# A four-layer network's attention keys: turned and split into three parts one stage earlier

## The chip, the cores and the metric

The kernel runs on 1 core of one Trainium2 chip. The metric is device time in microseconds (us), the median of several executions. Work goes to five engines: TensorE (PE, its weight loads apart as PEld), VectorE (DVE), ScalarE (ACT), GpSimd (POOL) and SyncE (SP), which here only issues transfers. Each engine runs its own instructions in the order in which they are written, and waits on semaphores for the others.

## The reference, cut to what matters

x is 4 batches of 512 rows of 256 numbers. Four layers follow one another, each an attention over a context of 1601 rows and a feed-forward part.

```python
x = x + tanh(g_xattn[0]) * L0_xattn(layernorm(x), ctx)
x = x + tanh(g_ffn[0]) * quantised_linear(layernorm(x))
x = x + tanh(g_xattn[1]) * L1_xattn(layernorm(x), ctx, mask)      # keys and queries turned (RoPE)
x = x + tanh(g_ffn[1]) * L1_experts(layernorm(x))                 # 8 experts, relu
x = x + tanh(g_xattn[2]) * L2_xattn(layernorm(x), ctx, mask)
x = x + tanh(g_ffn[2]) * L2_experts(layernorm(x))                 # gelu
x = x + tanh(g_xattn[3]) * L3_xattn(layernorm(x), ctx)            # one wide head
x = x + tanh(g_ffn[3]) * L3_experts(layernorm(x))                 # selu, two experts a row
# attention of layers 1 and 2: 16 heads of 16
q, k, v = x @ Wq + bq, ctx @ Wk + bk, ctx @ Wv + bv
k = k * cos + rotate_half(k) * sin                                # layer 1 alone; q alike
attn = softmax(where(mask == 0, -big, q @ k.T * scale))
out = (attn @ v) @ Wo + bo
```

Keys and values hang on the context and on weights alone, so they can be computed before the layer that uses them begins.

## The kernel before

**Stages.** Each stage ends in a fence and its buffers are given back. In the profiled execution layer 1's stages are: the quantised linear part of layer 0 (928 to 1087 us), layer 1's attention (1087 to 2112), its experts (2112 to 2421), and then layer 2's attention (2421 to 3302).

**Keys made ahead.** `Prepared` belongs to a feed-forward stage. It projects keys and values of the next layer in 16 chunks of the context (4 batches of 512, 512, 512 and 65 columns; a chunk gives two pieces of keys of 128 rows, so 32 pieces in all). SP loads the context (L201), PE projects (L218 keys, L226 values), ACT moves the keys from PSUM to a ring of three buffers `p_kf` (L243) and stores them as float32 in DRAM (`keys`, L246). The chunks are put in parts; each engine's code names the place at which a part comes. `quantised_linear` has ten parts of one to seven chunks, the experts have three.

**Attention of layers 1 and 2** (`ready`). Scores are made in PE from bf16 operands: a float32 number is written as the sum of three bf16 parts (`split3`, four operations: L835 to L838), and the parts of q and k stand under one another in the rows of `qaug` and `kaug` (six runs of 16 rows, then four rows of mask, maximum and ones). So each piece of keys is loaded from `keys` (L725), and in layer 1 once more from `turned`, a copy in DRAM with the halves of each head swapped (L750, L778); POOL or DVE turns it (three operations, L860 to L862, with the table `turn`) and splits it; SP stores the three parts in `kparts` (L794), and only then fetches a group's operands to `kaug` (L816, six transfers of 16 partitions) and `qaug`.

**Groups and batches.** The 16 heads form four groups (g = 0 to 3) for each of four batches (b). `Plan` lays the order of all engines out as a list. `attend(g, b)` makes the 52 jobs of one group (13 key tiles times 4 heads: L1051 scores, L1143 exponential on ACT, L1062 product with v) and mixes into them what comes next: `maxima`, the pass over the scores for the maximum of each row (L1032 on PE, L930 on DVE, 32 steps a group, two groups ahead), `project` (queries L1007 and, before the change, all keys of the next batch, in groups 1 and 2), `fetch`, `take`, `normalise` and `output`. The end of a group is the copy `z<-pv` on ACT (L1150).

Of the kernel before, what the change touches and what calls it, by code (L numbers as in the profile page):

```python
# [14 lines left out]
H, HD = 16, 16  # L15
# [136 lines left out]
class Prepared:  # L152
# [3 lines left out]
    def __init__(self, kn, sb, w, slots, *counts):  # L156
        self.w, self.slots = w, slots
        self.wk, self.wv, self.bk = sb("p_wk", [P, DC, D]), sb("p_wv", [P, DC, D]), sb("p_bk", [P, DC])
        self.at, self.kf = sb("p_ctx", [P, 4, DC, 512]), sb("p_kf", [P, 3, 512])
        self.vb = sb("p_vb", [P, 2, 4, D])  # L160
        self.chunks, s, k = [], 0, 0
        for b in range(B):
            for n_c, (c0, n) in enumerate(CHUNKS):
                c = dict(b=b, n_c=n_c, i=len(self.chunks), keys=[], values=[])
                for j in range(DC):
                    c["keys"].append((j, s, k))
# [5 lines left out]
                self.chunks.append(c)  # L172
        self.n, self.n_keys = s, k
        self.parts, first = [], 0
        for n in counts:
            self.parts.append(self.chunks[first:first + n])
            first += n
        self.parts.append(self.chunks[first:])
        self.loaded = 0

    def ended(self, part):

        return self.parts[part][-1]["end"]


def prepare_weights_sp(kn, p):
# [18 lines left out]

def prepare_pe(kn, p, part):
# [3 lines left out]
    for c in p.parts[part]:  # L210
# [3 lines left out]
        for j, s, _ in c["keys"]:  # L214
# [16 lines left out]
def prepare_act(kn, p, part):  # L231
    act, p_full, p_free, p_w = kn.nc.scalar, kn.sema("p_full"), kn.sema("p_free"), kn.sema("p_w", DMA)
    keys, values = kn.dram["keys"], kn.dram["values"]
    many = len(p.slots)
    act.wait_ge(p_w.sem, p_w.at(3))
    for c in p.parts[part]:
        c0, n = CHUNKS[c["n_c"]]
        for j, s, k in c["keys"]:
            kept = kn.sema(f"p_k{k % 3}", DMA)
# [3 lines left out]
            act.activation(p.kf[:, k % 3, 0:n], p.slots[s % many][:, 0:n], ACT.Identity,  # L243
                           bias=p.bk[:, j:j + 1]).then_inc(p_free.sem, 1)
            act.wait_ge(p_free.sem, p_free.at(s + 1))
            act.dma_start(keys[c["b"], P * j:P * j + P, c0:c0 + n], p.kf[:, k % 3, 0:n]).then_inc(kept.sem, DMA)  # L246
# [11 lines left out]

def prepare_close(kn, p):

    n = len(p.chunks)
    for name, k in (("p_full", p.n), ("p_free", p.n)):
        kn.sema(name).close(k)
    kn.sema("p_w", DMA).close(3)
    for f in range(4):
        kn.sema(f"p_ctx{f}", DMA).close(n // 4)
    names = []
    for k in range(3):
        kn.sema(f"p_k{k}", DMA).close(len(range(k, p.n_keys, 3)))
        names.append(f"p_k{k}")  # L270
    for k in range(2):
# [22 lines left out]
class Unit:  # L294
# [13 lines left out]
    at: int = 0  # L308


class Plan:
# [16 lines left out]
    def add(self, kind, **f):  # L328
# [3 lines left out]
        if kind in ("q", "k"):  # L332
            if kind == "q" or not self.ready:
                u.s = self.next("s", 2 if self.rope else 1)
# [3 lines left out]
            u.at = self.next(f"kl{u.f}") if kind == "k" and self.ready else -1  # L338
# [34 lines left out]
    def split(self, kind, b, c, n_c, engines):  # L373
        n = self.next("split")
        self.add(kind, b=b, j=c, k=n_c, by=engines[n % len(engines)], f=n % (3 if n < 10 else 2))
# [86 lines left out]
    def lay_out_ready(self):  # L462
        lead, n = self.lead, 0
        self.add("begin", b=0, what="kvq")
        for n_c in range(len(CHUNKS)):
            for c in range(DC):
                self.split("k", 0, c, n_c, ("pool",) if n < (4 if self.rope else 5) else ("dve",))
                n += 1
        self.add("ln")
        for c in range(DC):  # L470
            self.split("q", 0, c, 0, ("pool",) if self.rope else ("dve",))
        for g in range(NG):
            self.add("fetch", b=0, g=g, what="k", k=1, by=f"kd{g}")
            if g == 0:
                self.add("fetch", b=0, g=0, what="q", k=NG, by="qd")
# [7 lines left out]
        self.attend(0, 0, (self.chain(self.maxima(1, 0, lead), self.maxima(2, 0, 0, lead)), MAX_STEPS, 0, JOBS - 1))  # L483
        for b in range(B - 1):
            peaks = (self.chain(self.maxima(2, b, lead), self.maxima(3, b), self.maxima(0, b + 1), self.maxima(1, b + 1),
                                self.maxima(2, b + 1, 0, lead)), MAX_STEPS, 0, JOBS - 1)
            projected = self.chain(self.project(b + 1, ("pool", "pool", "dve") if self.rope else ("pool",), "kvq"),
                                   *(self.then("fetch", b=b + 1, g=g, what="kq", k=1, by=f"kd{g}") for g in (0, 1)))
            self.attend(1, b, peaks, (projected, 6, 0, JOBS - 1), (self.normalise(0, b), 2, 2 * HG, JOBS - 1))
            self.attend(2, b, peaks, (projected, 6, 0, 36), (self.normalise(1, b), 2, 2 * HG, JOBS - 1))  # L490
            self.attend(3, b, peaks, (self.chain(self.then("fetch", b=b + 1, g=2, what="kq", k=1, by="kd2"),
                                                 *(self.then("take", b=b + 1, g=g) for g in range(3))), 4, 8, 24),
                        (self.normalise(2, b), 2, 2 * HG, JOBS - 1))
            self.attend(0, b + 1, peaks, (self.chain(self.then("fetch", b=b + 1, g=3, what="kq", k=1, by="kd3"),
                                                     self.then("take", b=b + 1, g=3)), 2, 8, 24),
                        (self.chain(self.normalise(3, b), self.output(b)), 2 + TT + 1, 2 * HG, JOBS - 1))
        peaks = (self.chain(self.maxima(2, B - 1, lead), self.maxima(3, B - 1)), MAX_STEPS, 0, JOBS - 1)
        for g in range(1, NG):
            self.attend(g, B - 1, peaks, (self.normalise(g - 1, B - 1), 2, 2 * HG, JOBS - 1))
# [13 lines left out]
def head_attention(kn, w, gate, scale, rope, mask, ready):  # L513
# [3 lines left out]
    with ctx:  # L517
# [8 lines left out]
        if rope is not None:  # L526
            a.wqr, a.bqr = sb("wqr", [P, DC, D]), sb("bqr", [P, DC])
            a.turn = sb("turn", [P, 2, 2, 512])
# [23 lines left out]
        if ready:  # L552
            a.fill = sb("fill", [R_ALL - R_MASK, S2], BF16)
            third = sb("third", [P, 3, 512], BF16)
# [5 lines left out]
        a.split_at.append((a.e_t[:, 0, 0, :], a.e_t[:, 0, 1, :], third[:, :, :]))  # L560
# [33 lines left out]
def head_sp(kn, a):  # L594
# [7 lines left out]
    turned = [sig(f"turn{f}", DMA) for f in range(2)]  # L602
# [3 lines left out]
    a.ctx_of, a.turn_of, a.arrived, a.stored_of = {}, {}, {}, {}  # L606
    ctx_until, turn_until = [None] * 4, [None] * 2
# [96 lines left out]
def head_ready_sp(kn, a, n_of):  # L704
# [4 lines left out]
    stored = [sig(f"stored{f}", DMA) for f in range(3)]  # L709
    turned = [sig(f"turn{f}", DMA) for f in range(2)]  # L710
    split = {n: sig("split_" + n) for n in ("pool", "dve")}
    v_taken, vl, swapped = sig("v_taken"), sig("vl", DMA), sig("swapped", DMA)
    keys, turn_keys, values = kn.dram["keys"], kn.dram["turned"], kn.dram["values"]
# [1528 lines left out]
```

## Time and profile before

| | |
|---|---|
| median of 3 executions | 4383.25 us (4382.84 to 4405.29) |
| the profiled execution's own time | 4430.76 us |
| its span | 4429.5 us |
| mean granted clock of PE | 0.903 of full speed |
| PE busy | 3646.0 us (82%) |
| DVE busy | 2172.4 us (49%) |
| ACT busy | 2069.1 us (47%) |
| POOL busy | 722.6 us (16%) |

The span is the stretch that the trace covers; the time is the same execution's from outside. Busy time of an engine says how much it has to do, the waits say who sets the pace at a place.

### The profile page before, as it was taken

To read this page: it belongs to the slowest core of one execution; us is meant where nothing else is said; L and a number is where in the kernel's file an instruction comes from. 1 tells how busy PE (TensorE), PEld (TensorE's weight loads), DVE (VectorE), ACT (ScalarE), POOL (GpSimd) and SP (SyncE) were. 2 spreads that over 40 slices of the span, in tenths; PEclk is the share of its full clock that TensorE was granted. 3 is DMA by queue.
4 is the path that set the end of the run, shared out by engine and by line. 5 is a ranking of instruction groups with operands and counts; after the bars stand their busy time and mean duration, and the time that the engine had idled before them with its cause. 6 is when DMAs were issued, how large, how long until landed. Compare 5 with 4: busy or idle time off the path is not lost. (4 is left out here: it accounts for less than half of the span.)

```text
span 4429.5 us, 54375 instructions
## 1 busy us (share of the span) xinstructions
PE 3646.0 (82%) x19494; PEld 1930.1 (44%) x19494; DVE 2172.4 (49%) x3371; ACT 2069.1 (47%) x4542; POOL 722.6 (16%) x732
## 2 busy tenths in 40 slices
PE   3999999988187879799898498898988978893993
PEld 2334343345022323233696133332337855583993
DVE  4766666632285767674202676676731121252332
ACT  1566666643034546466232165565653322252662
POOL 1112120011423131200202130312001100003013
PEclk8999999999578989899898598998999999996997
DMA  6242415034644343420755624434117521022555
GB/s 129 42 61 48 69 41 67 1 131 152 154 90 73 73 74 69 81 29 1 259 184 160 108 66 54 90 67 67 16 60 246 167 97 55 17 90 94 180 181 105
DMA packets 255284, 415.17 MB, mean 94 GB/s; under 512 B 51578, under 2 KB 169043, under 8 KB 252971
## 3 DMA queue, kind: packets, MB, share of 16 engines
q1 hardware_dynamic: 207714, 273.76, 29.1%
q0 software_dynamic: 27360, 98.58, 7.2%
q10 hardware_dynamic: 19944, 39.36, 2.3%
q8 instruction: 159, 2.61, 0.3%
q14 instruction: 107, 0.87, 0.1%
HBM read 305.62 MB, written 111.08 MB: 94 GB/s over the span
## 5 line engine op out<-in xcount | busy, mean ns | idle before, releaser
L1143 ACT ACTIVATE e_t<-s 128x512 f32<-128x512 f32 (+1 forms) x2496 | 1355.0, 599 | 981.3 <-PE s L1051 980.3
L930 DVE TENSOR_REDUCE mxp<-m 128x1 f32<-128x802 f32 x1536 | 1451.8, 987 | 666.0 <-PE m L1032 661.0
L1032 PE MATMUL m<-kaug,qaug 97*128 97x401 bf16 x3072 | 839.5, 357 | 281.4 <-DMA qaug<-qparts 91.7
L1051 PE MATMUL s<-qaug,kaug 100*128 100x512 bf16 (+1 forms) x2496 | 881.3, 394 | 34.3 <-DMA qaug<-tm 19.5
L1062 PE MATMUL pv<-e_t,v 128*32 128x512 f32 (+1 forms) x4992 | 686.3, 623 | 0.2
L1032 PEld LDWEIGHTS m<-kaug,qaug 97*128 97x128 bf16 x3072 | 281.8, 101 | 699.4 <-DVE mxp L930 253.3
L1051 PEld LDWEIGHTS s<-qaug,kaug 100*128 100x128 bf16 (+1 forms) x2496 | 238.9, 102 | 730.0 <-ACT e_t L1143 474.5
L1952 PE MATMUL y<-w,hT 128*128 (+1 forms) x1504 | 346.6, 385 | 11.6 <-DVE hT L1807 11.6
L1952 PEld LDWEIGHTS y<-w,hT 128*128 128x128 f32 x1504 | 283.2, 193 | 48.7 <-issue 6.4
L1943 PE MATMUL h<-xtT,w 128*128 128x128 f32 x2496 | 293.4, 276 | 4.8 <-issue 3.5
L1943 PEld LDWEIGHTS h<-xtT,w 128*128 128x128 f32 x2496 | 286.6, 193 | 6.1 <-issue 3.9
L893 POOL TENSOR_TENSOR r<-ones,rc 128x512 f32<-128x512 f32 x48 | 50.3, 1048 | 1343.6 <-DVE rc L952 1343.6
L1812 DVE SCALAR_TENSOR_TENSOR y<-y,b 128x256 f32<-128x256 f32 x94 | 39.5, 420 | 358.1 <-PE y L1952 358.1
L1062 PEld LDWEIGHTS pv<-e_t,v 128*32 128x32 f32 (+1 forms) x4992 | 99.5, 109 | 225.1 <-ACT e_t L1143 146.1
L2020 ACT ACTIVATE ez<-h,b 128x128 f32<-128x128 f32 x440 | 119.8, 387 | 158.2 <-PE h L1943 158.2
L1806 DVE TENSOR_SCALAR ez<-ez 128x1024 f32<-128x1024 f32 x55 | 38.2, 694 | 299.4 <-ACT z L2020 299.4
L836 POOL TENSOR_TENSOR kr<-kf,ks 128x512 f32<-128x512 f32 (+1 forms) x91 | 92.5, 1016 | 366.4 <-ACT ks L1119 361.3
L2025 ACT ACTIVATE hT<-h,b 128x128 f32<-128x128 f32 x312 | 84.7, 382 | 125.2 <-PE h L1943 125.1
L1767 POOL DMA_DIRECT2D w<-in_L_w x78 | 55.3, 708 | 504.8 <-PE h L1943 479.2
L2020 ACT ACTIVATE z<-h,b 128x128 f32<-128x128 f32 x440 | 122.5, 453 | 0.0
L218 PE MATMUL h<-p_ctx,p_wk 128*128 128x512 f32 (+1 forms) x256 | 107.7, 569 | 15.7 <-DMA p_ctx<-in_ctxT 14.6
L226 PE MATMUL h<-p_wv,p_ctx 128*128 128x256 f32 (+1 forms) x416 | 102.7, 397 | 20.7 <-ACT p_kf L243 11.6
(288 smaller groups left out, 3405.0 us busy)
## 6 DMA issues: line engine op xcount, KB each, us to landing
w<-in_L_w POOLq DMA_DIRECT2D x78, 1024.0 KB, 5.4
kaug<-kparts SPq DMA_DIRECT2D x276, 200.1 KB
kparts<-ks SPq DMA_DIRECT2D x66, 384.0 KB, 3.5
w<-in_L_w SPq DMA_DIRECT2D x24, 1024.0 KB, 13.3
p_ctx<-in_ctxT SPq DMA_DIRECT2D x36, 512.0 KB
keys<-p_kf ACTq DMA_DIRECT2D x72, 256.0 KB
values<-p_vb ACTq DMA_DIRECT2D x36, 512.0 KB
qaug<-qparts SPq DMA_DIRECT2D x216, 64.0 KB
```

The lines of the kernel that those rows point to most:

```text
L218: m = pe.matmul(p.slots[s % many][:, 0:n], p.wk[:, kc, P * j:P * j + P], p.at[:, f, kc, 0:n], start=kc == 0, stop=kc == DC - 1)
L226: m = pe.matmul(p.slots[s % many][0:KW[t], 0:D], p.at[:, f, kc, k0:k0 + KW[t]], p.wv[:, kc, :], start=kc == 0, stop=kc == DC - 1)
L836: kn.settle(eng, own, eng.tensor_tensor(rest, src, parts[0], ALU.subtract))
L930: dve.tensor_reduce(a.mxp[:, u.g % 2, half, n:n + 1], a.m_slot[u.m % 2][:].rearrange("p (a n) -> p a n", a=2)[:, :, 0:PIECE + 1], AX.XY, A ...
L1032: m = pe.matmul(slot[:, 512 * k:512 * k + PIECE + 1], a.qaug[0:R_MAX, u.g, j, P * qc:P * qc + P], a.kaug[0:R_MAX, u.g, j, k0:k0 + PIECE + ...
L1051: pe.matmul(slot[0:KW[u.k], :], a.kaug[0:R_ALL, u.g, u.j, P * u.k:P * u.k + KW[u.k]], a.qaug[0:R_ALL, u.g, u.j, :], start=True, stop=True) ...
L1062: m = pe.matmul(a.pv[32 * j:32 * j + 32, :], a.v[0:KW[u.k], u.k, u.g, VW * j:VW * j + 32], a.e_t[0:KW[u.k], u.n % 2, j, :], start=u.k == 0 ...
L1143: act.activation(a.e_t[0:KW[u.k], e % 2, u.j, :], a.s_slot[u.s % 3][0:KW[u.k], :], ACT.Exp).then_inc(s_free.sem, 1)
L1943: m = pe.matmul(a.h_slot[i % 2][:, P * f:P * f + P], a.w1[:, w1_at, c, P * f:P * f + P], xT(c), start=c == 0, stop=c == DC - 1)
L1952: m = pe.matmul(a.y_slot[i % 2][:, 0:D], a.hT[:, i % 2, f, :], w2(f), start=f == 0, stop=f == FC - 1)
L2020: t = act.activation(to[:, p, P * f:P * f + P], slot[:, P * f:P * f + P], func, bias=bias(f))
L2025: t = act.activation(a.hT[:, p, f, :], slot[:, P * f:P * f + P], func, bias=bias(f))
```

## The change

The turn and the split move from the attention of layers 1 and 2 into the stage ahead of each. There ACT evicts keys to a ring of four and no longer stores them. For layer 1 SP swaps halves from `p_kf` to `p_kr` within SBUF (L236 of the changed kernel), POOL and DVE turn and split in `prepare_split` (L335 to L337 and L876 to L879, seven operations a piece), and SP stores the three parts to `kready` (L242). So that halves are 64 partitions each, the columns of Wk are permuted on the host; the fetch to `kaug` then takes pieces of 8 partitions in layer 1 (twelve transfers of a group) and stays at six of 16 in layer 2. For layer 2 there is no turn, and ACT writes the first part. The 42 transfers that clear `xs` come six after each part instead of all at once. In the attention the key loads, turns, splits, stores and the swapped copies in DRAM are gone; each group's operands of the next batch are fetched and taken within the next group (`renew`), and queries alone are projected, on POOL's split.

```diff
@@ Prepared, prepare_sp (new: a part at a time)
-def prepare_sp(kn, p, upto):
+def prepare_sp(kn, p, part):
...
+    def swap(x):
+        swapped = kn.sema(f"p_sw{x['k'] % p.RING}", DMA)
+        sp.wait_ge(p_free.sem, p_free.at(x["s"] + 1))
+        f, n = x["k"] % p.RING, x["cols"]
+        for r in (0, P // 2):
+            sp.dma_start(p.kr[r:r + P // 2, f, 0:n], p.kf[P // 2 - r:P - r, f, 0:n]).then_inc(swapped.sem, DMA)
+
+    def store(x):
+        split, kept = kn.sema("p_split_" + x["by"]), kn.sema(f"p_k{x['k'] % p.RING}", DMA)
+        sp.wait_ge(split.sem, split.at(x["n"] + 1))
...
+    for c in p.parts[part]:
+        prepare_load_sp(kn, p, min(c["i"] + 4, len(p.chunks)))
+        if p.in_parts:
+            for x in c["keys"]:
+                if p.rope is not None:
+                    swap(x)
+                held.append(x)
+                if len(held) > 2:
+                    store(held.pop(0))
+    for x in held:
+        store(x)
@@ prepare_act
-            if k >= 3:
-                act.wait_ge(kept.sem, kept.at(k // 3))
+            if k >= p.RING:
+                act.wait_ge(kept.sem, kept.at(k // p.RING))
@@ prepare_split (new, on POOL and DVE)
+        if p.rope is not None:
...
+            eng.tensor_tensor(src, src, p.turn[:, 0, c0:c0 + n], ALU.mult)
+            kn.settle(eng, own, eng.tensor_tensor(o, o, p.turn[:, 1, c0:c0 + n], ALU.mult))
+            kn.settle(eng, own, eng.tensor_tensor(src, src, o, ALU.add))
+        split3(kn, eng, own, kn.cst["ones"][:, 0:1].to_broadcast([P, n]), o, src, [p.ks[:, f, k, 0:n] for k in range(3)],
+               p.rope is None).then_inc(done.sem, 1)
@@ quantised_linear, quant_sp, quant_dve
+        both = ("pool", "dve")
+        a.p = Prepared(kn, sb, ahead, [s[:] for s in a.p_slot], True, rope,
+                       ((1, ("pool",)), (1, ("pool",)), *((1, both) for _ in range(7)), (7, both)))
-    for n in range(XTILES):
-        sp.dma_start(kn.dram["xs"][P * n:P * n + P, :], a.zero[:]).then_inc(zeroed.sem, DMA)
-    prepare_sp(kn, a.p, len(a.p.chunks))
+    for part in range(len(a.p.parts)):
+        prepare_sp(kn, a.p, part)
+        for n in range(min(XTILES, 6 * part), min(XTILES, 6 * part + 6)):
+            sp.dma_start(kn.dram["xs"][P * n:P * n + P, :], a.zero[:]).then_inc(zeroed.sem, DMA)
@@ experts
-            a.p = Prepared(kn, sb, ahead, [s[:, 512 * i:512 * i + 512] for s in a.h_slot for i in range(2)], 1, 6)
+            a.p = Prepared(kn, sb, ahead, [s[:, 512 * i:512 * i + 512] for s in a.h_slot for i in range(2)], kind == "relu", None,
+                           ((2, ("pool",)), (5, ("dve",)), (9, ("dve",))))
@@ Plan.lay_out_ready
+        for g in range(2):
+            self.add("fetch", b=0, g=g, what="k", k=1, by=f"kd{g}")
+        self.add("begin", b=0)
+        for g in range(2, NG):
+            self.add("fetch", b=0, g=g, what="k", k=1, by=f"kd{g}")
...
+        for b in range(B):
+            on = b + 1 < B
+            queries = [(self.project(b + 1, ("pool",), "q"), 3, 8, 24)] if on else []
+            self.attend(0, b, peaks, *last, *queries)
...
+            for g in range(1, NG):
+                renew = [self.renew(g - 1, b + 1)] if on else []
+                self.attend(g, b, peaks, *renew, (self.normalise(g - 1, b), 2, 2 * HG, JOBS - 1))
...
+    def renew(self, g, b):
+
+        return self.chain(*(self.then(k, b=b, g=g, what="kq", k=1, by=f"kd{g}") for k in ("fetch", "take"))), 2, 6, 28
@@ head_ready_sp, fetch
+                        for t in range(2):
+                            r = r0 + HD // 2 * t
+                            sp.dma_start(a.kaug[r:r + HD // 2, u.g, :, :], piece(keys[u.b, k])[c, t, :, h:h + HG, :]).then_inc(by.sem, DMA)
```

On SP, the whole rest of the quantised stage after its weights and first loads stood like this before (`xs<-zero` clears, `p_ctx` are context chunks):

```order
L201 DMA p_ctx<-in_ctxT 128x2x65
L1453 DMA xs<-zero 128x256 x42
L201 DMA p_ctx<-in_ctxT 128x2x512 x3
L201 DMA p_ctx<-in_ctxT 128x2x65
L201 DMA p_ctx<-in_ctxT 128x2x512 x3
```

In the changed kernel the same place on SP reads:

```order
L222 DMA p_ctx<-in_ctxT 128x2x65
L236 DMA p_kr<-p_kf 64x512 x4
L242 DMA kready<-p_ks 128x3x512 x2
L1490 DMA xs<-zero 128x256 x6
L222 DMA p_ctx<-in_ctxT 128x2x512
L236 DMA p_kr<-p_kf 64x512 x4
L242 DMA kready<-p_ks 128x3x512 x2
L1490 DMA xs<-zero 128x256 x6
L222 DMA p_ctx<-in_ctxT 128x2x512
```

The swap of a part now stands behind the stores of the part before it and its six clears; it is so for nine parts of one chunk, seven of them with clears behind them.

On SP, at the start of layer 1's attention, the changed kernel first fetches the keys of groups 0 and 1 (twelve transfers each), loads the weights of the queries and the table,, and then, up to the fetch of the queries (`fill` are constant rows, `vn` the values, `qready` the queries' parts), has:

```order
L817 DMA qaug<-fill 1x16x512
L821 DMA woa<-in_L_woa 128x1024
L821 DMA bva<-in_L_bva 128x4
L821 DMA bob<-in_L_bo 128x256
L801 DMA vn<-values 128x3072
L802 DMA vn<-values 65x256
L851 DMA kaug<-kready 8x4x1601 x12
L858 DMA kaug<-maskrow 1x4x1601
L851 DMA kaug<-kready 8x4x1601 x12
L858 DMA kaug<-maskrow 1x4x1601
L827 DMA qready<-ks 128x3x512 x2
L844 DMA qaug<-qready 16x16x512 x6
```

Before, the last of the key pieces and the fetches stood there:

```order
L730 DMA kr<-turned 128x65
L794 DMA kparts<-third 128x3x512
L738 DMA turn<-in_rope 128x2x512
L794 DMA kparts<-ks 128x3x65 x2
L794 DMA qparts<-third 128x3x512
L794 DMA qparts<-ks 128x3x512
L816 DMA kaug<-kparts 16x4x1601 x6
L820 DMA kaug<-maskrow 1x4x1601
L816 DMA qaug<-qparts 16x16x512 x6
L816 DMA kaug<-kparts 16x4x1601 x6
```

In front of these rows before stand all loads, turns and splits of eight key pieces; in the changed kernel the first thing is two fetches, and the queries' fetch stands behind four groups of keys instead of behind one.

## Rows read from the trace of the kernel before

**Rows 1.** Windows of the stages (us, busy time (x instructions) by engine, PEclk, DMA share, GB/s)

```profile
928.00:1087.00 159.00, 136.87 (x532) 93.56 (x532) 53.93 (x112) 55.76 (x118) 22.10 (x10) 0.96 0.51 166
...
1087.00:1213.00 126.00, 18.66 (x48) 9.72 (x48) 33.84 (x79) 11.44 (x24) 59.51 (x53) 0.56 0.68 170
...
2421.00:2497.00 76.00, 16.53 (x41) 7.54 (x42) 37.95 (x72) 10.47 (x22) 29.04 (x29) 0.52 0.75 144
```

**Rows 2.** Waits of PE in layer 1's attention (total us, times, longest)

```profile
PE m L1032 <- DMA qaug<-qparts: 49.9, 1, 49.9
...
PE m L1032 <- DVE mxp L930: 42.0, 30, 8.4
...
PE m L1032 <- DMA kaug<-maskrow: 28.4, 3, 14.6
...
PE s L1051 <- DMA qaug<-tm: 10.3, 3, 3.7
```

**Rows 3.** Waits of PE in layer 2's attention

```profile
PE m L1032 <- DMA kaug<-maskrow: 24.9, 3, 8.6
```

**Rows 4.** Timeline of ACT, ends of groups in both attentions (start us, us, engine line op)

```profile
1302.65 0.58 ACT L1150 COPY z<-pv 128x512 f32<-128x512 f32 x1 [0.76 <-PE pv L1062]
...
2095.74 0.58 ACT L1150 COPY z<-pv 128x512 f32<-128x512 f32 x1 [1.19 <-PE pv L1062]
...
2586.22 0.58 ACT L1150 COPY z<-pv 128x512 f32<-128x512 f32 x1 [0.76 <-PE pv L1062]
...
2628.29 0.59 ACT L1150 COPY z<-pv 128x512 f32<-128x512 f32 x1 [0.76 <-PE pv L1062]
...
2735.06 0.59 ACT L1150 COPY z<-pv 128x512 f32<-128x512 f32 x1 [0.77 <-PE pv L1062]
...
2784.31 0.58 ACT L1150 COPY z<-pv 128x512 f32<-128x512 f32 x1 [0.77 <-PE pv L1062]
...
3173.24 0.58 ACT L1150 COPY z<-pv 128x512 f32<-128x512 f32 x1 [0.76 <-PE pv L1062]
...
3285.75 0.58 ACT L1150 COPY z<-pv 128x512 f32<-128x512 f32 x1 [1.19 <-PE pv L1062]
```

**Rows 5.** Group of line 1007, layer 2, half the queries of one batch (ns min/median/max, first, last start)

```profile
L1007 PE MATMUL s<-xnT,wq x4: 590/592/593, 2641.2 to 2642.5; 128*128 128x512 f32 x4
```

**Rows 6.** Timeline of POOL and DVE in layer 1's attention, before its first maximum

```profile
1102.49 1.38 POOL L860 TENSOR_TENSOR kf<-kf,turn 128x512 f32<-128x512 f32 x1 [6.17 <-DMA turn<-in_rope]
...
1111.08 1.26 POOL L860 TENSOR_TENSOR kf<-kf,turn 128x512 f32<-128x512 f32 x1
...
1144.06 1.70 POOL L860 TENSOR_TENSOR kf<-kf,turn 128x512 f32<-128x512 f32 x1
...
1153.63 1.48 POOL L838 TENSOR_TENSOR ks<-kr,ks 128x512 bf16<-128x512 f32 x1
...
1141.55 1.53 DVE L861 TENSOR_TENSOR kr<-kr,turn 128x512 f32<-128x512 f32 x1
```

**Rows 7.** Windows, transfers into 4 partitions and into 16 (columns as in the first group)

```profile
36.00:38.00 2.00, 2.00 (x12) 1.50 (x10) 1.18 (x3) 1.84 (x6) 0.00 (x0) 1.00 0.25 26
...
1194.00:1204.00 10.00, 0.00 (x0) 0.00 (x0) 0.00 (x0) 0.00 (x0) 0.00 (x0) 0.50 1.12 118
```

**Rows 8.** DMA issues 1087 to 1213 us (count, KB each, median us to landing)

```profile
kaug<-kparts SPq DMA_DIRECT2D x24, 200.1 KB
...
qaug<-qparts SPq DMA_DIRECT2D x6, 256.0 KB, 15.2
```

**Rows 9.** Timeline of ACT, POOL, DVE and SP in the quantised stage

```profile
940.26 0.69 ACT L243 ACTIVATE p_kf<-p,p_bk 128x512 f32<-128x512 f32 x1 [1.02 <-PE p L218]
...
971.66 2.34 POOL L1466 TENSOR_TENSOR t<-t,xh 128x1024 f32<-128x1024 f32 x1 [33.98 <-DVE t L1509]
...
963.92 1.22 DVE L1500 TENSOR_REDUCE sc<-xh 128x4 f32<-128x1024 f32 x1 [7.97 <-ACT xh L1597]
...
932.32 23.98 SPq L1453 DMA_DIRECT2D xs<-zero  x42
```

More of the change, by code:

```diff
@@ L172, in __init__ @@
                 self.chunks.append(c)
+                part.append(c)
+            self.parts.append(part)
         self.n, self.n_keys = s, k
[L174 to L178, printed above, removed]
+        self.keys = [x for c in self.chunks for x in c["keys"]]
         self.loaded = 0
@@ L183, in ended, with keys_of @@
         return self.parts[part][-1]["end"]
+    def keys_of(self, part):
+        return [x for c in self.parts[part] for x in c["keys"]]
 def prepare_weights_sp(kn, p):
@@ L213, in prepare_pe @@
         pe.wait_ge(arrived.sem, arrived.at(c["i"] // 4 + 1))
-        for j, s, _ in c["keys"]:
+        for x in c["keys"]:
+            j, s = x["j"], x["s"]
             if s >= many:
@@ L267, in prepare_close @@
     names = []
-    for k in range(3):
-        kn.sema(f"p_k{k}", DMA).close(len(range(k, p.n_keys, 3)))
+    for k in range(p.RING):
+        many = len(range(k, p.n_keys, p.RING))
+        kn.sema(f"p_k{k}", DMA).close(many)
         names.append(f"p_k{k}")
+        if p.rope is not None:
+            kn.sema(f"p_sw{k}", DMA).close(2 * many)
     for k in range(2):
@@ L307 @@
     last: bool = False
-    at: int = 0
 class Plan:
@@ L462, in lay_out_ready @@
     def lay_out_ready(self):
[L463 to L468, printed above, removed]
+        lead = self.lead
+        for g in range(2):
[3 more added lines that the diff above has]
+            self.add("fetch", b=0, g=g, what="k", k=1, by=f"kd{g}")
         self.add("ln")
         for c in range(DC):
[L471 to L475, printed above, removed]
+            self.split("q", 0, c, 0, ("dve", "pool"))
+        self.add("fetch", b=0, g=0, what="q", k=NG, by="qd")
         for _ in self.maxima(0, 0):
@@ L482, in lay_out_ready @@
             pass
[L483 to L496, printed above, removed]
@@ L708, in head_ready_sp @@
     s_full, m_free, td, ld, rows, filled = sig("s_full"), sig("m_free"), sig("td", DMA), sig("ld", DMA), sig("rows", DMA), sig("filled")
-    stored = [sig(f"stored{f}", DMA) for f in range(3)]
-    turned = [sig(f"turn{f}", DMA) for f in range(2)]
     split = {n: sig("split_" + n) for n in ("pool", "dve")}
-    v_taken, vl, swapped = sig("v_taken"), sig("vl", DMA), sig("swapped", DMA)
-    keys, turn_keys, values = kn.dram["keys"], kn.dram["turned"], kn.dram["values"]
+    stored = [sig(f"stored{f}", DMA) for f in range(2)]
@@ L800, in head_ready_sp @@
         elif u.kind == "fetch":
             by = sig(u.by, DMA)
-            for f in range(3):
-                if a.dmas.get(f"stored{f}"):
-                    sp.wait_ge(stored[f].sem, stored[f].at(a.dmas[f"stored{f}"]))
-            if u.b == 0 and u.g == 0 and "k" in u.what:
-                sp.wait_ge(rows.sem, rows.at(2))
+            if "q" in u.what:
+                for f in range(2):
+                    sp.wait_ge(stored[f].sem, stored[f].at(u.b + 1))
             if u.b:
@@ L1467, in quant_pool @@
         pool.tensor_tensor(a.xq[:, u, :, :], q, h, ALU.add).then_inc(xq_made.sem, 1)
+        if i == 0:
+            split(2)
+        elif i < QN - 1:
+            split(2 * i + 1)
+            split(2 * i + 2)
+    for part in (7, 8, 9):
+        split(part)
 def quant_dve(kn, a):
@@ L1514, in quant_dve @@
             quantised(i + 1)
+            split(3 + 2 * i)
         for h in range(2):
@@ L1519, in quant_dve @@
                                      ALU.add).then_inc(y_free.sem, 1)
+        split(4 + 2 * i if i + 1 < QN else 9)
 def quant_pe(kn, a):
```

300 lines of the change are left out of this document (158 added, 142 removed).

## The prediction

> **What bounds the kernel now.** The table of windows comes first, cut at the stages and at the first maximum of each attention [rows 1]. Between the fence and the first maximum of layer 1's attention lie 126 us in which PE is busy for 18.7, and 76 us in layer 2's with 16.5; the DMA share there is 0.68 and 0.75. These stretches are the work on keys (loads, turns, splits, stores) and then fetches. In the quantised stage PE is busy for 137 of 159 us, DVE for 54 and POOL for 22: PE bounds it, and two engines stand idle, so that is where the change puts the work.
>
> Next, what PE waits for after that. In layer 1 it waits once for 49.9 us for the queries' parts, 42.0 us in 30 waits for DVE's maxima, 28.4 us in three waits for a group's keys and 10.3 us for `tm` [rows 2]; in layer 2 the three waits for keys are 24.9 us [rows 3]. The waits for keys are the fetches that follow the last split of a batch, and those for maxima fall where DVE does splits besides. The ends of groups give the sizes: layer 1 takes 2095.7 − 1302.7 = 793 us from the end of its first group to that of its last (16 in all), layer 2 takes 3285.8 − 2586.2 = 699.5 [rows 4]. A group that meets none of this takes 2628.3 − 2586.2 = 42.1 us, the one that also projects the output 2784.3 − 2735.1 = 49.3, and the last three of a layer, which have less and less ahead of them, 3285.8 − 3173.2 = 112.5.
>
> **Gain in the steady part.** Keys are no longer loaded or split here, so I rebuild the 15 intervals from undisturbed groups. Nine (groups 1 to 3 of three batches) at 43, one above the 42.1 since a fetch and a take still stand in them: 387. Three first groups of a batch with the output: 49.3 each, two of them with a projection of queries. This costs PE (2642.5 − 2641.2) / 3 = 0.43 us a matmul [rows 5], so 16 matmuls in layer 1 (with the turned weights) 7 us, and 8 in layer 2 3.4 us. Sum for layer 1: 387 + 49.3 + 2 × 56.3 + 112.5 = 661.4; gain 793 − 661.4 = 131.6, less 7 for the projection that now stands in the very first group: 125. Layer 2: 387 + 49.3 + 2 × 52.7 + 112.5 = 654.2; gain 45.3, less 3.4: 42. DVE and POOL have no more splits of keys, so they can't be late for that; the new fetch is issued at the seventh job of a group, lasts up to 24 us (below), and its first reader, the `turn` and the next pass of maxima, comes about 37 us after the group's start. That hides it, with some 8 us to spare, and what it costs if that is used up is a rival.
>
> **The start of an attention.** The rate of a transfer here goes with the partitions it writes: into 4 partitions 26 GB/s, into 16 partitions 118 [rows 7]. Keys of a group are six pieces of 200.1 KB, 1.23 MB, queries six of 256 KB [rows 8]. At 118 GB/s keys take 10.5 us and queries 13.3. In layer 1 the pieces now have 8 partitions, for which no row stands. Between the two rates, in proportion (26 × 2 = 52, 118 / 2 = 59), I take 60: 20.5 us a group. All four groups stand ahead of the queries: 82 + 13.3, and with them the three constant rows (16 copies of 3.2 KB a row at 26 GB/s, 6.5), the values 5.3, the queries' stores 2.6, weights and table 6, latencies 4: 120 against 126, a gain of 6. Bounds: at 118 GB/s it is 40 less, a gain of 46; at 26 GB/s 8-partition pieces would give 4 × 47 us and a loss of 100, which nothing speaks for, since a rate that doubles and doubles again with the partitions would have to stay flat for one step. Layer 2 keeps 16 partitions: 42 + 13.3 + 6.5 + 5.3 + 2.6 + 2.3 + 0.9 + 4 = 77, against 76: nothing. The Trainium skill's "SBUF — State Buffer" (Door 1: The DMA port swizzle) lets a transfer's rate go with the number of 16 ports its partitions reach, four partitions to a port, 27.2 GB/s each. The two rows agree with it, at 26 and 118 against 27 and 109; by it 8 partitions get 54 GB/s, and the gain at this start would be about nothing.
>
> **The cost in the quantised stage.** A piece takes seven operations. On POOL alone that is 1111.1 − 1102.5 = 8.6 us; when DVE works beside it 1153.6 + 1.5 − 1144.1 = 11.0, and DVE's operations take 1.53 us each, so 7 × 1.53 plus gaps, about 11 as well [rows 6]. So two engines at once make a pair in 11.5 us, little better than POOL's 17.2 for two alone. Beside "SBUF — State Buffer" (Who interferes with whom) this is plain: the Trainium skill has DVE with two inputs in SBUF and GpSimd take turns on a shared port. The rows say the same with a number.
>
> SP goes through parts one by one, and each step waits for the one before: swap (two transfers of 64 partitions, issue and landing, 2.9), the pieces, stores (0.9), six clears at 23.98 / 42 = 0.57 us each, 3.4 [rows 9]. The second piece is evicted at 941 us [rows 9], so the chain begins at about 945 with the table loaded. The parts:
> parts 0 and 1, both pieces on POOL: 2 × (17.4 + 2.9 + 0.9 + 3.4) = 49;
> parts 2, 4, 5, 6 (full, shared): 4 × (11.5 + 7.2) = 75; part 8, without clears, 15;
> parts 3 and 7 (65 columns): 10 + 7;
> between them DVE's `quantised` (963.9 to 971.7, 7.7 us) and POOL's two operations of 2.34 [rows 9] three times on the chain, 12.4 less the 7.2 in which SP is busy anyway: 16;
> the last part of seven chunks, swaps ahead of the pieces: 5 full pairs × 11.3 + 2 small pairs × 2.6 + 4 for the ring of four: 66;
> landing of the last store 3.
> 945 + 49 + 75 + 15 + 17 + 16 + 66 + 3 = 1186, against 1086.5: **100 us longer**. PE's own work (137 us) is no longer the bound, it is held by the ring.
> Bounds: if the chain were only POOL's share with swaps and clears hidden (14 full pieces × 8.6, 4 small ones × 2.6 and 19 for the quantised operations, from 945), the end is at about 1096: +10. With every swap 4 us later behind values and context loads and no overlap in the last part it is +140. Both are far, and the chain above is written in SP's order, so I take 100.
>
> **The experts of layer 1.** One chunk more stands ahead of the routing and one less behind; DVE splits ten pieces while it has nothing else until the first tile, and 18 in its gather, where it is mostly idle. POOL's four pieces end before the scatter. I allow 5 us for the input loads that now queue behind the last stores of part 1 on SP; bounds 0 and 15.
>
> **Sum.** 125 + 42 + 6 + 0 − 100 − 5 = 68 us of the profiled execution's 4430.8, 1.5%. The median before is 4383.25, 1.1% under that execution, so 4383.25 × (1 − 68 / 4430.8) = **4316 us**.
>
> **Rivals.** Faster by more: (B) 8-partition fetches run at 118 GB/s, since sixteen DMA engines may work on several pieces at once. Then −40: 4276. It speaks for it that SP issues the pieces apart; against it that 4-partition fills in a row stay at 26 [rows 7]. (C) The quantised stage costs 60 or less, since swaps and clears overlap with pieces and DVE is no slower when POOL merely stores: 40 us less, 4276, with B 4236. (E) Within 0.5%: new waits take 40% of the steady gain, as the 8-partition fetches of 24 us meet `tm` (already 3.5 us a time [rows 2]) and the queries' splits on POOL: 67 us back, 4383. (D) Slower: the chain on SP is longer than worked out. Each swap needs both halves landed and stands in the queues behind stores, values and clears; if it comes 4 us later in nine parts (36), if the last part is serial too (5 × 7 = 35) and `quantised` is slowed by POOL from 7.7 to 13 four times (21), the stage is 192 longer: 4383 + 92 − 68 = 4407. The mechanism is this one chain; it decides from 168 us on (100 + 68), and makes the kernel more than 0.5% slower from 190 on. That the changed keys don't save anything because PE bounds the groups anyway is excluded by the ends of groups: 793 / 15 = 52.9 us on average in layer 1 beside 42.1 undisturbed [rows 4].
>
> **Chances.** 0.5%, about 22 us, is what a measurement can tell from no change: borders 4361 and 4405. A as worked out, 4290 to 4350: 0.40. B 0.12. C (with or without B) 0.20. E 0.15. D 0.13. A to C make faster 0.73 with a little of their sides, same 0.15, slower 0.12. The range leaves out 2 in 10: 4235 at C with B, up to 4390 past E.
>
> **What the profile would show.** Of the changed kernel: groups of 43 us in both attentions, with waits for `kaug<-maskrow` gone and those for maxima under 10 us; first maximum of layer 1 about 120 us after its fence, of layer 2 77; 8-partition fetches near 60 GB/s in a stretch in which nothing else moves; a quantised stage of 259 us in which POOL is busy for most and PE for half, its parts 18 to 19 us apart; the experts' stage within 5 us of 309. Wrong would be the prediction if parts follow one another in 12 us or in 25, if the 8-partition rate is 118, or if groups still take 50 us and more.

## The result, and the profile after

The changed kernel takes 4316.3 us (median of 4, 4315.4 to 4318.2), the kernel before beside it 4386.1 (4382.8 to 4405.3): a ratio of 0.983 [0.980, 0.986], 70 us less. On a second chip it was 4317.5 against 4385.8, 0.984 [0.980, 0.989]. The kernel before took from 4370 to 4431 us over the chips used here. The changed one took 4314 to 4323, but it was timed on two chips only, and on both of them the kernel before has its median at 4386. The profiled execution after took 4315.6 us (span 4314.4, clock 0.917), the one before 4430.8, so the two traces lie 115 us apart, 45 more than the medians. Which chip the trace of before comes from is not on record. A table by stage (us), cut at the first instruction of each norm, the first maximum and the ends of groups:

| stretch | before | predicted change | after | measured change | after, second trace |
|---|---|---|---|---|---|
| quantised stage | 158.7 | +100 | 268.2 | +109.5 | 266.2 |
| layer 1: fence to first maximum | 126.5 | −6 | 80.5 | −46 | 87.0 |
| layer 1: first maximum to last end of a group | 89.5 + 793.1 | −125 | 95.7 + 652.7 | −134.2 | 96.4 + 652.6 |
| layer 1's experts | 308.8 | +5 | 329.5 | +20.7 | 325.7 |
| layer 2: fence to first maximum | 75.9 | 0 | 71.9 | −4 | 71.8 |
| layer 2: first maximum to last end of a group | 89.5 + 699.5 | −42 | 92.7 + 644.8 | −51.5 | 92.7 + 644.9 |
| layer 2's experts | 259.6 | 0 | 249.6 | −10 | 249.1 |
| sum | | −68 | | −115.5 | |

Windows of the changed kernel at the same stages as [rows 1] (columns as there):

```profile
927.00:1195.60 268.60, 159.95 (x532) 104.90 (x532) 179.22 (x209) 56.67 (x118) 167.76 (x135) 0.79 0.46 141
1195.60:1276.00 80.40, 16.10 (x48) 8.36 (x48) 21.02 (x59) 11.15 (x24) 16.13 (x17) 0.58 0.67 135
1276.00:2041.00 765.00, 716.90 (x3976) 255.34 (x3976) 533.48 (x695) 474.18 (x872) 71.93 (x64) 0.97 0.22 36
2041.00:2370.00 329.00, 289.17 (x1586) 239.49 (x1586) 92.95 (x242) 115.33 (x340) 66.36 (x68) 0.92 0.64 205
2370.00:2442.00 72.00, 12.34 (x40) 7.61 (x40) 17.96 (x55) 10.38 (x22) 12.13 (x14) 0.57 0.96 140
```

PE is busy for 160 of the 268 us of the quantised stage, 137 of 159 before: the same 532 matmuls at a granted clock of 0.79 instead of 0.96. DVE went from 54 to 179 us and POOL from 22 to 168. In the attention of layer 1 the answer to [rows 2] is (total us, times, longest):

```profile
PE m L1067 <- issue: 29.2, 1, 29.2
PE s L1042 <- DVE bqr L948: 24.8, 1, 24.8
PE s L131 <- DVE ot L118: 24.7, 1, 24.7
PE m L1073 <- DVE nm L879: 15.2, 16, 2.4
PE m L1110 <- DVE mxp L965: 6.0, 12, 0.5
PE m L1067 <- DVE mxp L965: 5.1, 20, 0.9
PE s L1086 <- ACT e_t L1178: 3.8, 14, 0.5
```

Nothing of `kaug`, `tm` or of `mxp` by 42 us is left: those waits for maxima are down to 5.1. Ends of groups of layer 1, the first two and the last, as [rows 4]:

```profile
1371.84 0.59 ACT L1185 COPY z<-pv 128x512 f32<-128x512 f32 x1 [0.76 <-PE pv L1097]
...
1413.91 0.59 ACT L1185 COPY z<-pv 128x512 f32<-128x512 f32 x1 [0.76 <-PE pv L1097]
...
2024.55 0.59 ACT L1185 COPY z<-pv 128x512 f32<-128x512 f32 x1 [1.19 <-PE pv L1097]
```

1413.9 − 1371.8 = 42.1, and so is every group 1 to 3. The first group of a batch is 56.1 in layer 1 (output and queries), 52.2 in layer 2, 49.2 with the output alone.

### The profile page after: what moved, and what is told of

Its sections match the earlier page's. It is cut to its first block and busy times, and to the rows that moved or that the text cites. A ratio compares the mean times of both kernels' runs of the same rounds, so it can differ in the third digit from the quotient of the medians.

```text
span 4314.4 us, 54207 instructions
## 1 busy us (share of the span) xinstructions
PE 3605.3 (84%) x19494; PEld 1934.2 (45%) x19494; DVE 2248.4 (52%) x3444; ACT 2083.9 (48%) x4574; POOL 643.0 (15%) x627
## 5 line engine op out<-in xcount | busy, mean ns | idle before, releaser
L1067 PE MATMUL m<-kaug,qaug 97*128 97x401 bf16 x3072 | 816.1, 348 | 159.1 <-issue 62.9
L1086 PE MATMUL s<-qaug,kaug 100*128 100x512 bf16 (+1 forms) x2496 | 858.6, 384 | 14.6 <-ACT e_t L1178 11.8
L1097 PE MATMUL pv<-e_t,v 128*32 128x512 f32 (+1 forms) x4992 | 667.3, 607 | 0.2
L1358 PE MATMUL s<-kT,qT 128*128 128x512 f32 (+1 forms) x256 | 98.8, 541 | 18.6 <-ACT e_t L1414 15.3
L280 PE MATMUL p<-p_wv,p_ctx 128*128 128x256 f32 (+1 forms) x208 | 60.8, 448 | 59.3 <-ACT p_kf L299 59.3
```

Source lines behind the costliest of these rows:

```text
L280: m = pe.matmul(p.slots[s % many][0:KW[t], 0:D], p.at[:, f, kc, k0:k0 + KW[t]], p.wv[:, kc, :], start=kc == 0, stop=kc == DC - 1)
L1067: m = pe.matmul(slot[:, 512 * k:512 * k + PIECE + 1], a.qaug[0:R_MAX, u.g, j, P * qc:P * qc + P], a.kaug[0:R_MAX, u.g, j, k0:k0 + PIECE + ...
L1086: pe.matmul(slot[0:KW[u.k], :], a.kaug[0:R_ALL, u.g, u.j, P * u.k:P * u.k + KW[u.k]], a.qaug[0:R_ALL, u.g, u.j, :], start=True, stop=True) ...
L1097: m = pe.matmul(a.pv[32 * j:32 * j + 32, :], a.v[0:KW[u.k], u.k, u.g, VW * j:VW * j + 32], a.e_t[0:KW[u.k], u.n % 2, j, :], start=u.k == 0 ...
L1358: m = pe.matmul(a.s_ps[:, c0:c0 + w], a.qT[:, c, P * k:P * k + P], a.kT[:, b % 2, c, c0:c0 + w], start=c == 0, stop=c == DC - 1)
```

## Experiments

**The kernel before again.** No edit.

> The kernel before, unchanged, profiled a second time. The traces of before and after differ by 115 us, the medians by 70, and the first trace of before belongs to an execution of 4430.8 us, 1% above its median. Theory 1 (that execution had chance delays in layer 1's attention, in the waits for DVE and DMA): this trace is 4383 to 4395 us, and the 40 us less are found between the first and the last end of a group in layers 1 and 2, which then take some 760 and 690 us and no longer 793 and 700. Theory 2 (whoever profiles this kernel slows it): again about 4430 us.

4420.2 us beside a median of 4422 of seven other executions on that chip (4410 to 4427); attention of layer 1 between ends of groups 792.1 us, of layer 2 691.0. Of the windows at its stages, the quantised stage, the start and the rest of layer 1's attention:

```profile
926.10:1086.30 160.20, 135.84 (x532) 92.58 (x532) 53.61 (x110) 55.77 (x118) 21.71 (x9) 0.96 0.51 164
1086.30:1210.70 124.40, 15.56 (x48) 8.09 (x49) 34.27 (x79) 11.41 (x24) 59.97 (x53) 0.57 0.67 172
1210.70:2109.50 898.80, 760.57 (x3976) 265.37 (x3976) 595.48 (x767) 475.72 (x872) 166.54 (x160) 0.89 0.33 61
```

These are the lengths of the first trace, 159, 126 and 899. So that trace was no accident, and Theory 1's place for the extra time is wrong. But Theory 2 doesn't hold either, since executions without a profile on that chip took the same. What differs between a chip where this kernel takes 4385 and one where it takes 4422 isn't shown: no execution near 4385 has a trace.

One stage tells chips apart, though. Layer 2's experts take 259.7 us here and 257.0 to 262.8 in the three edits of the changed kernel that ran on this chip (pieces of 8 partitions in layer 2, DVE alone, pieces held), but 249.1 to 251.8 in the versions of the changed kernel with the same plan of chunks on other chips. The first trace of before has 259.6. On the one chip that has traces of both kernels this stage doesn't change, so the −10 of that row of the table most likely goes with the chip and not with the change.

**The changed kernel again**, on one chip with three edits below: weights ahead of the keys, one chunk ahead of the routing, a later fetch.

> The changed kernel unchanged, timed on the same chip as the three below and the kernel before. Theory 1 (the kernel before is the one that scatters, from 4383 to 4427 us over the chips so far, since its attention waits for transfers): the changed kernel stays within 10 us of 4316, and the ratio to before is 0.975 to 0.983. Theory 2 (chips differ for both alike): 0.983 and 4345 us.

4317.5 us (4314.5 to 4322.5) against 4385.8 (4370 to 4408). The time is the one that Theory 1 gave, and 0.984 is a hair above its ratio. But the kernel before took on this chip what it took on the first one (4386), so the two theories were not told apart: the changed kernel as it stands was never timed where the kernel before takes 4422. The nearest to it is the next run, on that chip. It differs in the keys of layer 2 alone, which cost it 8 us, so the changed kernel would take about 4328 there (an estimate, 4336.6 − 8.4), 94 less than 4422. By that it follows the chips too, by 11 us where the kernel before moves by 36.

**Layer 2's keys in pieces of 8 partitions.**

```diff
-                        sp.dma_start(a.kaug[r0:r0 + HD, ...], keys[...].rearrange("(h d) k -> d h k", d=HD))
+                        for t in range(0, HD, HD // 2):
+                            sp.dma_start(a.kaug[r0 + t:r0 + t + HD // 2, ...], keys[...].rearrange(...)[t:t + HD // 2])
```

> The changed kernel, but layer 2's keys too are fetched in twelve pieces of 8 partitions instead of six of 16. Theory 1 (the rate goes with a piece's partitions, 60 GB/s for 8, as the prediction took it): the first maximum of layer 2's attention comes some 40 us later, 1% on the whole. Theory 2 (several pieces are written at once and the rate of a group stays near 118 GB/s; the first maximum of layer 1 came 81 us after its fence): 0 to 5 us later.

4336.6 us (4326 to 4337), where the kernel before takes 4422. The first maximum of layer 2 came 80.3 us after the fence, against 71.9: 8 later, not 40 as in Theory 1, though more than the 0 to 5 of Theory 2. In the steady part the rate is lower, and yet its groups stay at 42.1 us, so the fetch is hidden at either rate. A window of the fetch of one group in layer 2, here:

```profile
2596.20:2602.20 6.00, 5.91 (x37) 1.84 (x34) 4.97 (x6) 4.23 (x8) 0.49 (x1) 1.00 0.53 70
```

and in the changed kernel, with 16 partitions:

```profile
2578.90:2584.90 6.00, 6.00 (x41) 2.62 (x40) 4.20 (x6) 3.84 (x8) 1.04 (x1) 1.00 1.07 119
```

70 GB/s at a DMA share of 0.53, and 119 at 1.07. Layer 1 of the changed kernel has 64 GB/s in such a fetch, and groups of 42.1 in spite of it:

```profile
1418.00:1430.00 12.00, 11.82 (x71) 3.81 (x72) 9.63 (x11) 8.99 (x17) 1.04 (x1) 1.00 0.54 64
```

In all of these fetches SP issues one piece of the queries (16 partitions) before every two pieces of keys.

**Weights and values ahead of the keys.**

```diff
-        for g in range(2):
-            self.add("fetch", b=0, g=g, what="k", k=1, by=f"kd{g}")
         self.add("begin", b=0)
-        for g in range(2, NG):
+        for g in range(NG):
             self.add("fetch", b=0, g=g, what="k", k=1, by=f"kd{g}")
```

> The changed kernel, but in the attention of layers 1 and 2 weights, constant rows and values are loaded ahead of all fetches of keys. The projection of the queries waited there until 41 us after the fence, for the last small load behind two groups of keys. Theory 1 (that wait sets the start, since the queries' splits, stores and fetch follow it in a row): the first maximum comes 8 to 15 us earlier in each attention, 15 to 30 us in all. Theory 2 (the start is bound by the bytes that all fetches move, whatever the order): 0 to 5 us.

4303.4 us (4281 to 4308) against 4317.5 on the same chip: 14 less, just under the 15 to 30 of Theory 1. The trace puts layer 1's start at 78.7 us against 87.0 for the changed kernel there, layer 2's at 71.0 against 71.8. So Theory 1 holds in layer 1 (8 us, of 8 to 15) and not in layer 2 (1 us). The ratio to before, 0.980 [0.974, 0.985], overlaps with the unedited change's 0.984 [0.980, 0.989], but all four executions lie below all four of the unedited change on that chip, so this gain is likely, not sure. Its trace has the cleanest view of the disputed rate, a stretch in which keys in pieces of 8 partitions and nothing else move:

```profile
1224.00:1236.00 12.00, 0.00 (x0) 0.00 (x0) 0.00 (x0) 0.00 (x0) 3.92 (x4) 0.50 0.52 123
```

123 GB/s, at the same DMA share of 0.52 as in the slow fetches of one group. That is not the one rate of a queue of pieces either. Two stretches at the start of layer 1 in the changed kernel, the first in the first 5 us of its fetches, when a single group has been issued (SP issues the second from 1201.0 on), the second with the last group under way; in both hardly anything but keys moves:

```profile
1197.00:1201.00 4.00, 0.00 (x0) 0.00 (x0) 4.00 (x13) 0.00 (x0) 1.60 (x8) 0.50 0.52 89
1243.00:1251.00 8.00, 3.89 (x10) 1.39 (x8) 6.61 (x7) 5.21 (x7) 3.22 (x3) 0.92 0.51 198
```

So pieces of 8 partitions have been seen at 64 (with some of the queries among them), 89, 123 and 198 GB/s, always at a share of 0.51 to 0.54.

**One chunk ahead of the routing.**

```diff
-                           ((2, ("pool",)), (5, ("dve",)), (9, ("dve",))))
+                           ((1, ("pool",)), (6, ("dve",)), (9, ("dve",))))
```

> The changed kernel, but in the experts of layers 1 and 2 one chunk is prepared ahead of the routing and six behind it, as in the kernel before. The stage of layer 1's experts measured 329.5 us, 20.7 more than before; the first scatter came 10 us later, the first tile 13. Theory 1 (the second chunk ahead of the routing delays it): the scatter is 7 to 10 us earlier, and the stage 7 to 10 shorter. Theory 2 (the stores and splits of the keys are what is late, SP's load of the first tile standing behind them): the stage stays within 3 us, since six chunks then stand between the routing and that load.

4309.6 us (4303 to 4313), 8 less than 4317.5, but the stage of layer 1's experts stayed at 325.4 against 325.7. Its first scatter and first tile:

```profile
2090.67 1.22 POOL L1809 DMA_INDIRECT xs<-xn,to_u  x1 [28.81 <-DVE to_u L1947]
...
2138.15 1.09 PE L2043 MATMUL b<-ident,xt 128*128 128x128 f32 x4 [9.16 <-DMA xt<-xs]
```

The stage began at 2043.8, so the scatter came 46.9 us into it (55.3 in the changed kernel on that chip), the tile 94.3 (93.1). That is Theory 2: what the scatter gained, the tile waited. The 5 us that the trace did gain are in layer 2's experts (243.9 against 249.1), which have the same plan and no splits.

**A later fetch.**

```diff
-    ... for k in ("fetch", "take"))), 2, 6, 28
+    ... for k in ("fetch", "take"))), 2, 28, 36
```

> The changed kernel, but the operands of a group of the next batch are fetched at job 28 of a group and no longer at job 6, some 18 us later, with 15 us left to the turn that the prediction put 37 us after a group's start. Theory 1 (a fetch in pieces of 8 partitions lasts up to 24 us): PE waits up to 10 us in each of twelve groups of layer 1, groups of 50 us. Theory 2 (it lasts some 12 us, the rate that the start of layer 1's attention showed): groups stay at 42.1 and the time within 10 us.

4340.8 us (4336 to 4352), 23 more. Layer 1 from first to last end of a group is 682.4 us against 652.7, layer 2 unchanged at 644.8. Neither theory: of the 15 intervals of layer 1 eleven are as long as before, and the loss stands in the first group of two batches (68.2 and 68.7 instead of 56.1) and the one behind each (44.4 and 44.7), where PE waited for `tm` twice:

```profile
PE s L1086 <- DMA qaug<-tm: 19.7, 2, 10.1
```

So a delay of 18 us is more than the cover of one fetch in a batch, in two of three batches, by some 10 us, and less than that of all others; the cover is there, and wider at most places than the 8 us that the prediction gave.

**DVE alone splits in the quantised stage.**

```diff
-                       ((1, ("pool",)), (1, ("pool",)), *((1, both) for _ in range(7)), (7, both)))
+                       (*((1, ("dve",)) for _ in range(9)), (7, ("dve",))))
+    split(0)
+    split(1)
     quantised(0)
```

> The changed kernel, but DVE splits all 32 pieces of the quantised stage and POOL none. Theory 1 (two engines at once block each other: a pair costs 11.5 us, and DVE alone takes 0.69 us an operation, so about 10 us a pair): the stage is 10 to 25 us shorter, also since parts 0 and 1 take 10 us a pair and no longer 17. Theory 2 (both engines' work adds up): a pair costs 22 us on one engine, the stage is over 80 us longer.

4314.6 us, and a stage of 250.3: 18 less than with both engines, on a chip where the plain change wasn't timed. The whole stage in one window:

```profile
925.70:1176.00 250.30, 160.80 (x532) 107.94 (x532) 190.20 (x335) 55.05 (x118) 22.31 (x10) 0.78 0.49 151
```

DVE is busy for 190 us here and for 179 when POOL takes 18 of the 32 pieces: POOL's 145 us of work (168 − 22) saved DVE 11. That is Theory 1. A pair of full pieces takes DVE alone 9.7 us (4.9 a piece), and the two engines side by side about 10.5 (rows further down). The other reason that Theory 1 gave, parts 0 and 1 on DVE and no longer on POOL, is worth little: the first piece of part 2 starts 69.2 us after the fence against 72.5, so 3 of the 18 us come from there and 15 from parts that both engines shared.

**POOL alone.** The same with "pool" in every place.

> The changed kernel, but POOL splits all 32 pieces of the quantised stage and DVE none. With DVE alone on the pieces the stage was 250 us, with both 268. POOL alone takes 8.6 us a full piece. Theory 1 (two engines share one way to SBUF, so what counts is one engine's own pace): 24 full pieces of 8.6 us and 8 small ones of 2.6 are 227 us, 19 us of quantised operations and the waits between parts come on top: a stage of 290 to 310 us, 20 to 40 more than with both. Theory 2 (both engines add up, nearly halving the time): 60 us more or beyond.

4373.4 us (4369 to 4377); the stage is 318.5, with POOL busy for 236:

```profile
925.90:1244.30 318.40, 171.54 (x532) 111.85 (x532) 78.58 (x110) 55.96 (x118) 236.24 (x233) 0.73 0.38 119
```

50 more than with both, above Theory 1's band and below Theory 2's. The engine's own pace (227 + 19) is met, the rest are the waits between parts. The order is DVE 250, both 268, POOL 318.

**Two pieces held from part to part.** SP swaps the next part before it stores this one.

```diff
-    held = []
+    held = p.held
...
-    for x in held:
-        store(x)
+    if p.rope is None or part == len(p.parts) - 1:
+        while held:
+            store(held.pop(0))
```

> The changed kernel, but SP keeps two pieces held from one part to the next, so the swap of a part is issued ahead of the stores and clears of the part before it. Theory 1 (the chain swap, pieces, stores, clears on SP sets the quantised stage): each of nine parts loses the 6 to 7 us of swap and clears from its chain, so the stage is 40 to 60 us shorter, 4260 to 4275 in all. Theory 2 (the two engines' work on pieces and quantised sets it): less than 15 us.

4287.4 us (4284 to 4291), the stage 230.9 us: 37 less, just under Theory 1's 40 to 60 and far above 15. The time is above Theory 1's 4260 to 4275; it is 30 under that of the change as made, on another chip, and 41 under the 4328 estimated above for this one. DVE and POOL do the same work as before it (178 and 166):

```profile
924.00:1155.00 231.00, 158.06 (x532) 104.07 (x532) 177.94 (x209) 56.30 (x118) 165.71 (x136) 0.82 0.53 164
```

**Both of them.**

> The changed kernel with both edits of the quantised stage at once: two pieces held from part to part on SP (alone: stage of 231 us), and DVE splits all pieces (alone: 250 us). Theory 1 (the gains are of different things, the chain on SP and the blocking of DVE by POOL): DVE is busy for 190 us and the chain hides behind it, stage of 205 to 215 us, 4265 to 4275 in all. Theory 2 (with the chain relaxed two engines are worth having): 231 us or more.

4267.5 us (4267 to 4275), the stage 215.4, a little over Theory 1's 205 to 215. DVE is now busy for 193 of it:

```profile
926.00:1141.50 215.50, 149.95 (x532) 101.59 (x532) 193.16 (x335) 55.31 (x118) 23.25 (x10) 0.85 0.57 176
```

The gains of 37 and 18 add up to 55, and 53 were measured (268.2 − 215.4): the chain on SP and the blocking are two costs.

**The edits together, with DVE alone (all four) and with both engines (the three others).**

> All four edits that gained or were even: pieces held, DVE alone, weights ahead of the keys in the attention, one chunk ahead of the routing. If they add up on 4317: less 55 for the stage, 14 for the order and 8 for the experts, 4240; if the last two overlap with nothing but each other's scatter, 4245 to 4260.

> The same four edits without the third: both engines split. By the single runs 4317 less 30 for holding, 14 and 8: 4265. It decides between the engines' plans: Theory 1 has it 15 us or more above the version with DVE alone, Theory 2 has the two within 5 us.

4245.5 us (4232 to 4262; 0.966 of before [0.963, 0.969]) and 4256.9 (4244 to 4283; 0.970 [0.967, 0.974]), with the kernel before at 4394 on that chip. The quantised stages take 213.9 and 227.8. The stage keeps the 14 us of DVE alone, but the second version starts layer 1's attention 14 us sooner (65.3 against 79.6). The medians lie 11 us apart, between the 15 of Theory 1 and the 5 of Theory 2, and the intervals overlap, so which is faster in all stays open. They beat the kernel before by 3.4% and 3.0%, and stand 72 and 61 us under the change as made, on another chip. These versions scatter by 30 and 39 us, and the one with weights ahead of the keys by 27, so eight executions of the change as made within 8 us don't show that it scatters less than the kernel before.

## Why the prediction was right

The time was forecast as 4316 and is 4316.3; the fall of the medians 67 and is 70. But by its own steps this is good luck in part. The sum was set against the profiled execution, where 68 stand against 115. Scaling it to the median let the gain shrink by 1% with the base, but 115 us lie between the two traces and 70 between the medians. The sum was too small and the execution that it was taken from too slow, and the two errors met. The terms, one by one:

**The steady part** was right in mechanism and in size: 125 and 42 predicted, 134 and 51.5 measured. Groups 1 to 3 came at 42.1 and not at the 43 that I allowed for a fetch and a take, which makes 8 of the 9 us that it was short of in either layer. Keys' waits [rows 3] and waits for maxima [rows 2] went together, as worked out.

**The start of layer 1's attention** is the term that failed: a gain of 6 was taken, 46 measured, which is rival B. (The second trace has 39.5, and the runs that left this stretch alone had starts of 78 to 96 us, so gains of 30 to 48.) The step was "between the two rates, in proportion, I take 60". At the start the pieces of 8 partitions move at 89, 123 and 198 GB/s in the three stretches shown, and at 64 to 70 only in the fetch of one group in the steady part. Several groups in the queue are not what it takes, since the 89 were reached with one group issued; what the slow fetches have and the fast ones lack is pieces of the queries between those of the keys, and full work on the other engines. No run separates these. By the Trainium skill's "SBUF — State Buffer" (Door 1: The DMA port swizzle), which the prediction quoted, the estimate is 54 GB/s; the fetch in the steady part is near that, the start 1.6 to 3.7 times as fast. In all of them the DMA share is 0.51 to 0.54, about eight of sixteen engines; with 16 partitions it is 1.07. That eight engines fill more ports when they stand at different pieces would explain it; this was argued, not tried. Nor is the start bound by these fetches alone: with weights and values ahead of them it was 8 us shorter.

**The quantised stage** was 109.5 us longer against 100. The chain of SP is there, as these rows show, parts 2 to 4:

```profile
1010.42 0.91 SPq L242 DMA_DIRECT2D kready<-p_ks  x2
1011.38 3.69 SPq L1490 DMA_DIRECT2D xs<-zero  x6
1015.10 0.45 SPq L222 DMA_DIRECT2D p_ctx<-in_ctxT  x1
1015.60 2.42 SPq L236 DMA_DIRECT2D p_kr<-p_kf  x4
1025.86 0.91 SPq L242 DMA_DIRECT2D kready<-p_ks  x2
1026.81 2.95 SPq L1490 DMA_DIRECT2D xs<-zero  x6
1029.80 0.45 SPq L222 DMA_DIRECT2D p_ctx<-in_ctxT  x1
1030.30 2.43 SPq L236 DMA_DIRECT2D p_kr<-p_kf  x4
1043.92 0.91 SPq L242 DMA_DIRECT2D kready<-p_ks  x2
```

Part 4, a full one, takes 1043.9 − 1025.9 = 18.1 us, predicted 18.7, but the other full parts ahead of part 8 (2, 5 and 6) take 20.7 to 23.8. The two parts of 65 columns take 15.4 each and not 10 and 7; in part 3 the pieces wait for `quantised` on both engines. From the stores of part 1 to those of part 8 it is 131 us against 123 in the sum, and from there to the end 74 against 69; parts 0 and 1 took 3 less. That is the 9.5 us by which the term was short. A pair in part 4:

```profile
1033.43 1.27 POOL L335 TENSOR_TENSOR p_kf<-p_kf,p_turn 128x512 f32<-128x512 f32 x1 [7.60 <-DMA p_kr<-p_kf]
...
1042.41 1.48 POOL L879 TENSOR_TENSOR p_ks<-p_kr,p_ks 128x512 bf16<-128x512 f32 x1
...
1034.55 0.71 DVE L335 TENSOR_TENSOR p_kf<-p_kf,p_turn 128x512 f32<-128x512 f32 x1 [8.47 <-DMA p_kr<-p_kf]
...
1042.91 1.52 DVE L879 TENSOR_TENSOR p_ks<-p_kr,p_ks 128x512 bf16<-128x512 f32 x1
```

POOL takes 1042.4 + 1.5 − 1033.4 = 10.5 us for a piece and DVE 1042.9 + 1.5 − 1034.6 = 9.9, and six of DVE's seven operations 1.4 to 1.6 us each, where it needs 0.69 alone. The held pieces showed that 37 us of the stage go with the order of swaps and stores on SP, and DVE alone that 18 go with the split over two engines, 15 of them in shared parts.

**The experts of layer 1** cost 20.7 in the first trace and 16.9 in the second, not 5, which is past the bound of 15; against the second trace of before (312.2) it is 17.3 and 13.5. The step that failed says that only the input loads behind SP's stores cost something, 5. What stands there:

```profile
2196.43 0.66 PE L1984 MATMUL b<-ident,xt 128*128 128x128 f32 x4 [0.46 <-ACT p_vb L253]
```

in the kernel before, and after

```profile
2096.12 1.22 POOL L1809 DMA_INDIRECT xs<-xn,to_u  x1 [29.48 <-DVE to_u L1947]
...
2119.61 7.19 SPq L242 DMA_DIRECT2D kready<-p_ks  x4
...
2125.73 0.69 DVE L879 TENSOR_TENSOR p_ks<-p_kf,p_ks 128x512 bf16<-128x512 f32 x1
...
2126.85 19.25 SPq L1778 DMA_DIRECT2D xt<-xs  x5
...
2138.15 1.09 PE L2043 MATMUL b<-ident,xt 128*128 128x128 f32 x4 [12.10 <-DMA xt<-xs]
```

The scatter comes 55 us after the fence instead of 45, since the second chunk stands ahead of the routing, but with the scatter 8 us sooner the tile came no sooner. SP's queue decides: the load of the first tile stands behind the stores of part 1, and the last of these four needs the last split on DVE, which ends at 2126.4. So the load is issued 86.0 us into the stage (before, 67.3), and PE, done with its projections, waits for it for 12.1 us and not 0.5. Its first tile comes 97.3 us into the stage and not 84.4. The other 8 us lie behind that, 5 of them between the end of the last product on PE and the fence (62 against 57).

Layer 2's start and experts, −4 and −10, were taken at nothing; the −10 most likely goes with the chip, as said above.

Rival C (a stage of 60 or less more), D (190 more) and E (40% of the gain lost) did not occur. B did for its own term. Its 40 us, 19 of the steady part and the 14 of layer 2's rows, less 16 and 10 for the experts of layer 1 and the quantised stage, are the 47 by which the traces differ more than the sum, and the base that was too high by 45 took them back.

## What to carry to other kernels

Work that is moved off a bound engine to idle ones costs what its chain costs, not what the engines' busy time says: here 110 us of stage for 15 to 24 us a part, of which a third went with one reordering of swap and store. Two engines that each have two operands in SBUF are worth measuring against one: DVE alone was 18 us faster than DVE with POOL. And a sum worked out against one profiled execution should not be scaled to a median without a second trace of the same kernel, on the chip of the median: here one stage, alike in both kernels on one chip, differed by 10 us between chips.

## What the runs showed that was not expected

Pieces of 8 partitions move at 64 to 70 GB/s in the steady fetches of one group and at 89 to 198 at the start, at one and the same DMA share of 0.51 to 0.54; what sets the rate is open. DVE was busy for 11 us less in all when POOL did 145 us of the splits. And the kernel before takes from 4370 to 4431 us over chips.
